# A maximum over slots, taken by a tree of elementwise maxima instead of one strided reduction

## What is computed

```python
# layer 0
scores = jnp.where(A != 0, -arange(N), -inf)
vals, idx = jax.lax.top_k(scores, 25)
feats = jnp.where(valid[..., None], X[idx], -inf)
agg = feats.max(axis=2)
agg = jnp.where((degree <= 25)[..., None], jnp.maximum(agg, 0.0), agg)
out = relu(concatenate([X, agg], -1) @ W + b)
x = layernorm(x + out)
# layer 1: attention with 8 heads over the same neighbours, layer norm, elu
x = layernorm(x + L1(x, adj, ...))
```

## Time and profile before

| | |
|---|---|
| median of 3 runs | 3402.12 us (3399.23 to 3404.91) |
| span of the profiled execution | 3411.3 us |
| POOL busy | 2503.8 us, 73%, 2619 instructions |
| DVE busy | 2400.8 us, 70%, 5775 instructions |
| PE busy | 1642.6 us, 48% |
| ACT busy | 1115.1 us, 33% |
| DMA queues | 33.8% (issued by POOL) and 22.6% (issued by SP) of 16 engines' span |

### The profile page before, as it was taken

How to read it: one execution, slowest core, us unless ns; L and a number is a source line. 1 busy time by engine, 2 the same in 40 slices (tenths; PEclk the granted TensorE clock), 3 DMA queues, 4 the chain that set the end, 5 groups by cost and what they waited for, 6 DMA issues and landing times.

```text
span 3411.3 us, 25793 instructions
## 1 busy us (share of the span) xinstructions
PE 1642.6 (48%) x5249; PEld 1185.4 (35%) x5259; DVE 2400.8 (70%) x5775; ACT 1115.1 (33%) x2307; POOL 2503.8 (73%) x2619
## 2 busy tenths in 40 slices
PE   8046456443463435643555345544555434466454
PEld 1034334332342323432333233333433323344343
DVE  7798877567775677767695778767785465566666
ACT  3124343323333234332343334232232212223234
POOL 3576777777677776777777777777777777777775
PEclk9976667666666666666677666676676666677776
DMA  7667876655566556675666666555544444444332
GB/s 259 211 202 258 287 240 198 226 171 183 187 197 227 171 184 198 199 246 162 216 216 194 214 195 215 163 182 153 165 131 115 123 113 116 118 118 117 106 106 72
DMA packets 221587, 610.02 MB, mean 179 GB/s; under 512 B 68849, under 2 KB 112882, under 8 KB 194802
## 3 DMA queue, kind: packets, MB, share of 16 engines
q0 software_dynamic: 122880, 342.62, 33.8%
q1 hardware_dynamic: 98546, 265.71, 22.6%
HBM read 555.19 MB, written 52.95 MB: 178 GB/s over the span
## 4 chain that ended last, share of the span: by engine, by line
POOL 63%; issue 21%; DVE 9%; DMA 3%; DVEq 2%; PE 1%; ACT 1%; SPq 0%; POOLq 0%; ACTq 0%
POOL ring L618 54%; POOL out_dram L644 3%; POOL sorted_d L595 3%; DVE agg L1206 2%; DVEq L1028 2%; DVE cand L1067 2%; POOL table_d L637 1%; POOL pair_s L628 1%; DMA adj_i<-in_adj_dram 1%; PE att_p L921 1%; DVE cand L1083 1%; DMA ring<-sorted_d,idx_cur 1%; DMA table_d<-tab,idx_loc 0%; DVE agg L1196 0%; DVE adj_h L1063 0%
## 5 line engine op out<-in xcount | busy, mean ns | idle before, releaser
L618 POOL DMA_INDIRECT ring<-table_d,idx_loc x1096 | 1051.3, 959 | 354.1 <-issue 332.9
L618 POOL DMA_INDIRECT ring<-sorted_d,idx_cur x685 | 659.4, 963 | 208.8 <-issue 208.5
L893 PE MATMUL score_p<-ident,x1k 128*128 128x128 f32 x256 | 81.2, 418 | 1429.0 <-ACT x_t L721 1425.4
L921 PE MATMUL att_p<-ring,ident 128*128 128x256 f32 (+1 forms) x2384 | 605.8, 413 | 147.3 <-DVE ring L1363 146.6
L1206 DVE TENSOR_REDUCE agg<-ring 128x256 f32<-128x2560 f32 (+9 forms) x120 | 453.6, 3780 | 254.1 <-DMA ring<-sorted_d,idx_cur 184.8
L921 PEld LDWEIGHTS att_p<-ring,ident 128*128 128x128 f32 (+1 forms) x2384 | 499.9, 211 | 251.1 <-DVE ring L1363 135.7
L893 PEld LDWEIGHTS score_p<-ident,x1k 128*128 128x128 f32 x256 | 35.8, 197 | 1478.2 <-issue 1473.7
L752 ACT ACTIVATE neg<-z 128x256 f32<-128x256 f32 x128 | 53.3, 416 | 1471.9 <-DVE z L1249 1471.9
L618 POOL DMA_INDIRECT ring<-in_x_dram,idx_cur x411 | 395.2, 961 | 132.9 <-issue 124.4
L885 PE MATMUL lin_p<-w_s,h_t 128*128 128x256 f32 x1024 | 466.8, 635 | 0.0
L885 PEld LDWEIGHTS lin_p<-w_s,h_t 128*128 128x128 f32 x1024 | 316.5, 324 | 147.6 <-issue 80.6
(11 more groups left out here) (192 smaller groups left out, 2870.3 us busy)
## 6 DMA issues: line engine op xcount, KB each, us to landing
adj_i<-in_adj_dram SPq DMA_DIRECT2D x208, 1024.0 KB, 5.4
ring<-table_d,idx_loc POOLq DMA_INDIRECT x1096, 2.8
pay<-in_x_dram SPq DMA_DIRECT2D x8, 2048.0 KB, 9.6
xs<-sorted_d SPq DMA_DIRECT2D x128, 128.0 KB, 5.9
ring<-sorted_d,idx_cur POOLq DMA_INDIRECT x685, 2.8
table_d<-tab SPq DMA_DIRECT2D x80, 132.0 KB, 4.3
ring<-in_x_dram,idx_cur POOLq DMA_INDIRECT x411, 3.6
sorted_d<-pay,rank_i POOLq DMA_INDIRECT x128, 2.5
```

The costliest lines, as they stand in the source:

```text
L618: pool.indirect_dma_start(out=to[:, k * width:(k + 1) * width], out_offset=None, in_=source, in_offset=bass.IndirectOffsetOnAxis(ap=idx_at ...
L921: last = pe.matmul(att_p[:, 0:C], ident[0:on, :], r3[0:on, s, 0:C], start=(s == 0), stop=(s == k - 1))
```

## The change

The two reductions of tile 0 and the one of every other tile are replaced by a new function `halve`. While more than two slots are left, it takes the elementwise maximum of the first half of the slots and the last half, in place in the ring, and drains; of an odd number the middle slot stays. The last two slots are combined into the destination. For k slots it computes k - 1 slot-wide maxima: for 10 slots by instructions over 5, 2, 1 and 1 slots, for 16 over 8, 4, 2 and 1. Nothing is changed on the other engines.

```diff
+            def halve(rows, k, to):
+
+                while k > 2:
+                    h = k // 2
+                    v.tensor_tensor(rows[:, 0:h * C], rows[:, 0:h * C], rows[:, (k - h) * C:k * C], ALU.max)
+                    settle()
+                    k -= h
+                return v.tensor_tensor(to, rows[:, 0:C], rows[:, C:2 * C], ALU.max)
+
             def max_tile(i):
...
                 if u == 0:
                     unpack(rows, C)
-                    last = v.tensor_reduce(a, rows[:, 0:FULL * C].rearrange("p (k c) -> p c k", c=C), AX, ALU.max)
-                    settle()
-                    v.tensor_reduce(rprod[0:TOPS, 0:C], rows[0:TOPS, FULL * C:].rearrange("p (k c) -> p c k", c=C),
-                                    AX, ALU.max)
+                    last = halve(rows[:, 0:FULL * C], FULL, a)
+                    settle()
+                    halve(rows[0:TOPS, FULL * C:], SLOTS[0] - FULL, rprod[0:TOPS, 0:C])
                     settle()
                     last = v.tensor_tensor(a[0:TOPS, :], a[0:TOPS, :], rprod[0:TOPS, 0:C], ALU.max)
                 else:
                     if pair_of(0, i):
                         unpair(0, i, rows, C)
                         settle()
-                    last = v.tensor_reduce(a, rows.rearrange("p (k c) -> p c k", c=C), AX, ALU.max)
+                    last = halve(rows, SLOTS[u], a)
```

## The result

| | before | tree |
|---|---|---|
| median of 4 runs | 3400.68 us | 3462.96 us |
| span of the profiled execution | 3411.3 us | 3458.4 us |
| POOL busy | 2503.8 us | 2564.2 us |
| DVE busy | 2400.8 us | 2220.1 us |

A forecast was written before the change was run, and what follows sets the result against it. POOL's instruction count times their period was taken to bound the kernel. Holds of 98 us less 12 us of waits gave +86 us on the median of 3402.12, so 3488 us, with a range of 3445 to 3537 us.

The forecast's parts named there:

- What bounds: Whole kernel from 125 us on: time is POOL's instruction count times their period, 1.25 us for one gather each.
- The change on DVE: Reductions replaced by elementwise pieces: 20.4 us saved a graph, 163 us of DVE's 2400.8, nearly all off the path.
- The gain in waits: POOL's waits at 294, 339 and 1317 us: at most 15.0 us to gain, 12 us taken.
- The third item: POOL's 7.01 us wait at 1317 us: a faster DVE shortens it by 1.1 to 7.0 us, 4 taken.
- The coupling: POOL's gathers: an index read during a DVE instruction with two SBUF inputs waits for its end; 98 us added.
- The capped case: Rival on POOL's gathers: each read waits 0.37 us at most; +46 us, 3448 us; chance 0.10.
- the case of no hold: Rival on POOL's gathers: no extra hold, only waits shrink by 12 to 15 us; 3388 us; chance 0.09.
- a whole tree's hold: Rival: POOL isn't let in between pieces and waits for the whole tree; 295 us, 3685 us; chance 0.05.
- The size of the holds: Gathers under the trees: 12.3 us a graph, 98 us for eight, bounded by 0 and 135 us.
- the stepping: Estimate of holds: a read every 1.2525 us set against each tree from all phases; 1.73 us for tile 0.
- The check on the four short lines: Hold rule tested on L1241, L1249, L1315, L1330 of before: 34 us, 0.0134 us a gather, against 0.010 from mean and median.
- The sum: Whole kernel: 98 us of holds less 12 us of waits, +86 us, 3488 us, 2.5% slower; chance 0.76.

The follow-up runs named there:

- e3: Kernel before with reductions over 4 slots alone, other slots gathered but left out of the maximum; 3397.54 against 3405.3 us (0.9972).
- e4: Kernel before plus, per tile but tile 0, one 4-slot maximum with two SBUF inputs; 3464.35 against 3399.41 us (1.0187).
- e5: Kernel before plus, per tile but tile 0, a one-input reduction over 4 slots into a spare tile; 3415.11 against 3399.41 us (1.0050).
- e2: Tree's maxima taken slot by slot, running maximum in PSUM; 3411.18 against before's 3405.3 us on the second chip, 4183.57 against 4079.59 on the first.
- e8: The tree, unchanged, run again on the second chip; 3472.92 us against 3405.3 of the kernel before (1.0186).

## Why the prediction was right, and where its size was off

- **What bounds.** POOL's number of instructions times their period. Right: 279 us less of DVE bring 8 us (e3), 57 us more of POOL's busy time cost 49 us (e4 against e5).
- **The change on DVE.** 163 us saved were forecast, 180.7 measured as busy time. The forecast counts 328 drains at 0.07 us, 23 us, which busy time leaves out; with them it is 186 against 181. The pieces were right to 0.01 us but for those of one slot, 0.43 us where 0.41 stood.
- **The gain in waits.** 12 us forecast, 13.1 in the profile, and the nearness is in part luck. The 8.0 us at 294 and 339 went, as forecast. The third item was misread: the 7.01 us at 1317 are put down to PE, but POOL waits at that gather in every kernel, 6.21 us in the tree and 5.43 in e3 with 279 us less of DVE, so 0.8 us of it went where 4 were taken. What made up for it, 2.0 and 2.5 us of the two waits behind the earlier tables, wasn't in the forecast, and these three waits together lie anywhere between 12 and 21 us in the kernels here.
- **The coupling.** Right, and shown by e2 on the second chip, e4 and e5, though its condition was too narrow: the one-input copies of L1177 hold gathers as well. It reaches beyond the 0.69 us up to which the rows of before showed it: a 6-slot piece held a gather for 1.5 us, to its end. The capped case, the case of no hold and the case of a whole tree's hold are out. Single gathers of up to about 3 us, forecast under the 8-slot pieces, didn't come: the gathers began 0.8 to 1.2 us into those pieces, and the longest is 2.47 us, under a 6-slot piece.
- **The size of the holds**, the term that was mis-sized: 98 us forecast, 69 measured, summed over the timeline of the tree (what each gather that began during a tree took beyond its usual time), in some 135 gathers; the longest hold is 1.52 us. What failed is the step in which a piece holds for its whole length. A gather that starts less than about 0.05 us after a piece isn't held, and one that starts less than 0.13 us ahead of its end isn't either. The first edge, with the tree's 4-slot pieces of 1.23 us (the rows merge several pieces):

```profile
1358.24 2.06 DVE L1192 TENSOR_TENSOR ring<-ring 128x1024 f32<-128x1024 f32 x2
1358.27 0.94 POOL L618 DMA_INDIRECT ring<-table_d,idx_loc  x1 [0.30 <-issue]
```
```profile
1723.33 2.49 DVE L1192 TENSOR_TENSOR ring<-ring 128x1024 f32<-128x1024 f32 x3 [6.98 <-DMA ring<-sorted_d,idx_cur]
1723.39 1.97 POOL L618 DMA_INDIRECT ring<-table_d,idx_loc  x1 [0.30 <-issue]
```

0.03 us after the piece's start a gather keeps 0.94 us, 0.06 us after it takes 1.97. The second edge follows from the release: the gather ends 0.82 us after the piece and takes 0.95 alone, so only what remains of the piece beyond 0.13 us is lost. With 0.18 us taken off each piece the stepping gives for a graph 1.55 us (tile 0), then 0.95, 0.95, 0.69 three times, 0.44 four times, 0.31 twice, 0.26 twice, 0.13, 0.13: 8.7 us, 69 us for eight. That the total agrees so well is luck. Stepping supposes all phases alike, and they aren't: DVE starts a tree when a landing lets it, and 10 of the 16 six-slot pieces have a gather that begins 0.11 or 0.12 us after them and is held for 1.5 us. So tiles 1 were held 1.5 us each where stepping gives 0.95, tiles 0 1.3 where it gives 1.55, and tiles 3 0.5 where it gives 0.69. In the second execution of the tree (e8) the sum is 74 us. The rows of before held the clue. The check on the four short lines gave 0.0134 us a gather where 0.010 stood, and I took that as "a little high"; for pieces of 0.41 us the 0.18 us matter most, for the long ones less. The check was in fact further off: in the timeline of before the gathers under these four lines were held for 12 to 15 us in all, by how they are counted, where the rule gave 34, and much of the 0.010 comes from other lines, L1177 among them. The edges were found in the trace of the tree and then foretold the holds of e4 (52 us; summed over its timeline 53).
- **The sum.** 69 - 13 = +56 us by the mended terms, +62 measured, against +86 forecast; the range held it.

## What to carry to other kernels

Before an elementwise form replaces a reduction on DVE, ask who issues the gathers: if POOL does and bounds, every DVE instruction with two SBUF inputs costs it the rest of that instruction whenever an issue falls into it, and a copy within SBUF can do so too. Look at the spread of POOL's durations (mean against median) as well as at its busy share, and move one operand to PSUM where that costs nothing. And an engine with a 70% share can be worth 8 us out of 3400 if the other's instruction count sets the time.

## What was not expected of the hardware

That short pieces in a dense row hold POOL almost as much as long ones: its period stretched from 1.25 to 1.50 us, three pieces 0.50 apart, and the chain of one-slot pieces costs 61 us where the tree costs 68 on the same chip. Spread out, four such pieces a tile cost 18 us of POOL's time.

The hold runs the other way too, if for less: the two-slot piece at 743.19 in the tree, with a gather begun 0.02 us after its start, took 0.74 us where most take 0.69, and the gather kept 0.95.
